# SyncE's order of transfers around the rings and up tiles of a two-layer gated kernel

## What is computed

```
x  = L0_attn_x                                     # (8, 512, 256)
xn = layernorm(x)
s  = L0_attn(xn)   # 16 query heads, 4 key groups, causal, bias -slope*sqrt(i-j), softmax
g  = silu(L0_ffn(xn))     # silu(x@W1.T) * (x@W3.T), Walsh-Hadamard, @W2.T; 1024 hidden
x  = x + s * g
xn = layernorm(x)
s  = L1_attn(xn)   # 32 causal score maps of width 8; a1 - lam*a2, rms norm, @Wo.T
g  = silu(L1_ffn(xn))     # shared expert of 352 + 8 experts of 176, top 2 by sigmoid router
x  = x + s * g
```

## Time and profile before

| | |
|---|---|
| median of 3 runs | 2348.24 us (2347.73 to 2362.52) |
| profiled execution | 2355.72 us |
| its span | 2353.8 us |
| mean granted TensorE clock | 0.963 |
| TensorE busy | 2117.3 us (90%) |
| VectorE busy | 1372.4 us (58%) |
| ScalarE busy | 893.6 us (38%) |
| GpSimd busy | 683.5 us (29%) |
| up tiles: loads, median us to landing | 176, 3.9 |
| first layer's key rings: loads, median us to landing | 32, 7.2 |

### The profile page before, as it was taken

The page is one execution under the profiler, slowest core; times in us unless marked ns, Lnnn a source line. Parts: engine busy times, 40 slices in busy tenths (PEclk is TensorE's granted clock), DMA queues, the critical chain, the costliest instruction groups (busy, mean ns, idle before and its releaser), DMA issues.

```text
span 2353.8 us, 33709 instructions
## 1 busy us (share of the span) xinstructions
PE 2117.3 (90%) x12290; PEld 1437.2 (61%) x12386; DVE 1372.4 (58%) x2691; ACT 893.6 (38%) x1749; POOL 683.5 (29%) x845
## 2 busy tenths in 40 slices
PE   2299998999989999999989999999998999989898
PEld 1157556575666656676565755757556675656656
DVE  4465655656556565556647566475565666655664
ACT  2142451425424253333524345152451425433352
POOL 2332331313313233223323233141331323322331
PEclk7589999999999999999999999999999999999999
DMA  6823423243222533116231252323422253321530
GB/s 207 287 63 101 144 68 95 72 143 100 84 70 64 166 100 104 37 55 197 85 88 54 85 166 70 102 65 121 122 78 76 72 155 102 98 51 55 173 98 14
DMA packets 105604, 240.51 MB, mean 102 GB/s; under 512 B 17048, under 2 KB 27288, under 8 KB 105184
## 3 DMA queue, kind: packets, MB, share of 16 engines
q1 hardware_dynamic: 91184, 194.41, 27.4%
q0 software_dynamic: 14256, 43.94, 6.4%
HBM read 179.67 MB, written 57.82 MB: 101 GB/s over the span
## 4 chain that ended last, share of the span: by engine, by line
PE 63%; DMA 11%; DVE 7%; SPq 4%; ACT 4%; issue 3%; POOL 2%; DVEq 0%; ACTq 0%; POOLq 0%
PE bank L387 17%; PE bank L467 11%; PE bank L546 10%; PE bank L483 9%; PE bank L436 8%; DMA upring<-up_img 3%; DMA qring<-mneg 3%; DMA k_img<-probs 3%; PE bank L440 3%; PE bank L565 2%; ACT probs L624 2%; DMA kring<-k_img 2%; SPq L334 2%; SPq L351 2%; DVE nmax L718 2%
## 5 line engine op out<-in xcount | busy, mean ns | idle before, releaser
L718 DVE TENSOR_REDUCE nmax<-bank 128x1 f32<-128x512 f32 (+3 forms) x1056 | 651.3, 639 | 366.2 <-PE bank L440 353.7
L387 PE MATMUL bank<-xnT,upring 128*128 128x512 f32 (+1 forms) x2208 | 623.8, 405 | 24.6 <-DMA upring<-up_img 23.7
L624 ACT ACTIVATE probs<-bank 128x512 f32<-128x512 f32 (+1 forms) x864 | 469.1, 560 | 345.9 <-PE bank L467 331.8
L467 PE MATMUL bank<-qring,kring 128*128 128x512 f32 (+1 forms) x1056 | 478.2, 456 | 54.6 <-ACT probs L624 24.6
L436 PE MATMUL bank<-kring,qring 127*128 127x512 f32 (+3 forms) x1536 | 461.5, 353 | 50.9 <-DMA kring<-k_img 47.4
L387 PEld LDWEIGHTS bank<-xnT,upring 128*128 128x128 f32 x2208 | 396.4, 192 | 106.2 <-issue 33.5
L436 PEld LDWEIGHTS bank<-kring,qring 127*128 127x128 f32 x1536 | 272.9, 195 | 127.3 <-DMA kring<-k_img 50.3
L546 PE MATMUL bank<-wdown,hbuf 128*128 128x256 f32 x1408 | 338.9, 391 | 0.0
L467 PEld LDWEIGHTS bank<-qring,kring 128*128 128x128 f32 x1056 | 206.3, 197 | 189.2 <-ACT probs L624 100.1
L1494 POOL TENSOR_SCALAR_AFFINE_SELECT probs<-probs 128x512 f32<-128x512 f32 x256 | 163.2, 638 | 511.5 <-ACT probs L624 509.4
L546 PEld LDWEIGHTS bank<-wdown,hbuf 128*128 128x128 f32 x1408 | 267.6, 196 | 34.9 <-issue 1.7
(11 more groups left out here) (119 smaller groups left out, 1532.3 us busy)
## 6 DMA issues: line engine op xcount, KB each, us to landing
upring<-up_img SPq DMA_DIRECT2D x176, 512.0 KB, 3.9
q_img<-probs SPq DMA_DIRECT2D x96, 256.0 KB, 4.2
qring<-q_img SPq DMA_DIRECT2D x256, 64.0 KB, 1.9
kring<-k_img SPq DMA_DIRECT2D x64, 256.0 KB, 3.1
qring<-q_img SPq DMA_DIRECT2D x32, 384.0 KB, 4.9
k_img<-probs SPq DMA_DIRECT2D x48, 256.0 KB, 4.6
up_img<-hbuf POOLq DMA_DIRECT2D x22, 512.0 KB, 4.9
gring<-gate_img POOLq DMA_DIRECT2D x32, 256.0 KB, 3.7
```

Source lines behind the costliest of these rows:

```text
L387: last = nc.tensor.matmul(out_ap, part_a(a, pa, k), part_b(b, pb, k), start=(n == 0), stop=(n == len(steps) - 1))
L467: nc.tensor.matmul(SC[n % 2][:, 0:heads * w].rearrange("p (g n) -> p g n", g=heads), kring[l][:, ks, kt * P:(kt + 1) * P], qring[l][:, s, ...
L624: nc.scalar.activation(pr, pr if biased else scores, ACT.Exp, scale=scale).then_inc(s_exp, 1)
L718: nc.vector.tensor_reduce(nmax[:, u % 2, g0:g0 + heads, qt], MX[n % 2][:, 0:heads * w].rearrange("p (g n) -> p g n", g=heads), AX.X, ALU.m ...
```

## The change

SyncE's list is put in another order at two places, and two subtractions move from GpSimd to VectorE. In the front of every batch, up tile 11 is listed ahead of ring 4, image tiles 2 and 3 are listed apart from each other with up tile 12 between, ring 5 comes behind image 3, and the max row of unit 4 comes ahead of up tiles 14 and 15. In the seven tails, image tiles 0 and 1 are listed first, then ring 0, one up tile, image 2, rings 1 and 2, and the two other up tiles. The low parts of projections 0 and 1 of the next batch are made by VectorE ahead of its copy of projection 2; GpSimd makes that of projection 2. The wait for tile 21's linear half, once for the three up tiles, stands now in `up_load_next` at its first call. What is computed stays the same.

```diff
+        def up_load_next(sp, j):
+
+            if j == 0:
+                sp.wait_ge(s_u, so_far(s_u, J_ALL - 1))
+            sp.dma_start(upring[:, j].rearrange("p a h k n -> p (a h k n)").bitcast(F32), up_img[j]).then_inc(s_uppre[j], 16)
+
...
                 up_load(sp, FRONT_TILES[0] + 2)
                 write_images(sp, 1, (0, 1))
+                up_load(sp, FRONT_TILES[1] + 2)
                 ring_load(sp, UNITS[0])
-                up_load(sp, FRONT_TILES[1] + 2)
+                write_images(sp, 1, (2,))
+                up_load(sp, FRONT_TILES[2] + 2)
+                write_images(sp, 1, (3,))
                 ring_load(sp, UNITS[0] + 1)
-                up_load(sp, FRONT_TILES[2] + 2)
-                write_images(sp, 1, (2, 3))
-                for j in FRONT_TILES[3:-1]:
+                up_load(sp, FRONT_TILES[3] + 2)
+                max_row(sp, UNITS[0])
+                for j in FRONT_TILES[4:]:
                     up_load(sp, j + 2)
-                max_row(sp, UNITS[0])
-                up_load(sp, FRONT_TILES[-1] + 2)
                 if more_batches:
                     load_x(sp, slice((b + 1) * T, (b + 2) * T))
...
                 if more_batches:
-                    sp.wait_ge(s_u, so_far(s_u, J_ALL - 1))
-                    for j in range(UP_SLOTS):
-                        sp.dma_start(upring[:, j].rearrange("p a h k n -> p (a h k n)").bitcast(F32), up_img[j])\
-                            .then_inc(s_uppre[j], 16)
-                    write_images(sp, 0, range(3))
-                    for u in RINGS_AHEAD:
-                        ring_load(sp, u)
+                    write_images(sp, 0, (0, 1))
+                    ring_load(sp, 0)
+                    up_load_next(sp, 0)
+                    write_images(sp, 0, (2,))
+                    ring_load(sp, 1)
+                    ring_load(sp, 2)
+                    for j in range(1, UP_SLOTS):
+                        up_load_next(sp, j)
...
                 dve_linear_half(dve, TILE_AFTER[U_ALL - 1])
-                for i in range(3):
+                for i in range(2):
                     dve_project(dve, 0, i)
+                project_low(nc.vector, dve, 0, 0)
+                project_low(nc.vector, dve, 0, 1)
+                dve_project(dve, 0, 2)
                 dve_normalise(dve, U_ALL - 1)
...
                 if more_batches:
-                    for i in range(3):
-                        project_low(nc.gpsimd, pool, 0, i)
+                    pool.wait_ge(s_plo[0], so_far(s_plo[0], 2))
+                    project_low(nc.gpsimd, pool, 0, 2)
```

## The result

The changed kernel takes 2335.94 us in the median of 8 runs (2330.96 to 2345.82), the kernel before, in 8 runs beside it, 2347.98 (2339.72 to 2362.52). The ratio is 0.9938, with a 95% interval of 0.9918 to 0.9957. So it is faster by 12 us between the medians, or some 15 us by the ratio, where 61 were forecast.

A forecast was written before the change was run, and what follows sets the result against it. TensorE was taken as the bound, busy nine tenths; its waits and the slow clock behind them were worth 68 us at most. Front 19 + 6.7 and tail 21.2 + 14.0 made 61, from 2348.24 to 2287 us; range 2274 to 2318.

The forecast's parts named there:

- The tail: Seven tails: ring 0 lands 3.4 us earlier, winning 21.2 us of TensorE's ring stops and 14.0 of slow clock behind them.
- `kring` won 2.8 us for 2.5, and the images 1.4 for 0.9: Tail: ring 0 without image 2 ahead lands 2.5 us sooner; images without three up tiles ahead win 0.9.
- the 2.1 us of stops that were to stay: Tail: three of seven stops exceed the 3.4 us won, by 0.8, 0.4 and 0.9, so 2.1 us stay.
- the 4.7 of bytes spread over all engines: Tail, upper bound: if image bytes used all sixteen engines, images would win 4.7 us and every tail stop would vanish.
- The cover for the two low parts: Tail: VectorE's 2.40 us idle before the last unit's reciprocal covers two low parts, 1.4 us; uncovered, 10 us in all.
- The front: Eight fronts: of 23.7 us of up tile waits, 19 are won, plus 6.7 of slow clock.
- I take 2.4, because image 2 is issued right behind ring 4 and keeps the engines fed.: Front: up tile 11 fills 2.4 us of empty DMA time, so tile 13 lands 2.4 us earlier; lower bound 1.75.
- After: the same set, ring 5 moved from the middle to just ahead of it. No byte is saved.: Front: the same transfers stand ahead of tile 13, which gets 2.4 us earlier only because work starts in empty time.
- That adds 6.7: Front: with stops below 0.9 us the clock stays up, winning 1.7 us in four of eight fronts, 6.7 in all.
- The second one: Rival: the front keeps its stop at tile 13 and gives only 8 us, the tail 35; 2305 us, chance 0.22.
- The fourth rival: Whole change: closely following transfers slow each other and both landings stay; 5 to 20 us won, 2335 us, chance 0.12.
- The slower rival: Front: ring 4 waits in SyncE's queue behind up tile 11 and lands late; 2360 us, chance 0.02.

The follow-up runs named there:

- e2: The kernel before with only the tail's new order and the two low parts on VectorE, front as before; 0.9859 of the kernel before.
- e3: e2 with all three low parts left on GpSimd; 0.9858 of the kernel before.
- e1: The kernel before with only the front's new order, tail as before; 1.0080 of the kernel before.
- e8: e2 with one transfer moved, up tile 11 ahead of ring 4; 0.9865 of the kernel before.
- e10: e5 with up tile 11 moved back behind ring 4; 0.9799 of the kernel before.
- e5: The whole change, but with ring 5 behind up tile 13 instead of ahead of it; 0.9768 of the kernel before.
- e4: The whole change with GpSimd's first gate loads of a front held until tile 13's gate half is done; 0.9994 of the kernel before.
- e9: The whole change with the second of GpSimd's two front gate loads held until tile 11 is weighed; 0.9818 of the kernel before.

## Why the prediction failed

**The tail was right.** Forecast were 21.2 us of idle and 14.0 of slow clock, 35.2; the stage gave 35.7, and e2 alone 33. In the second batch `kring` won 2.8 us for 2.5, and the images 1.4 for 0.9, so that of the 2.1 us of stops that were to stay only 1.1 did. The images won 1.4 us and not the 4.7 of bytes spread over all engines. That agrees with the rule of the Trainium skill (DMA: Bandwidth & Descriptors, section "Why a DMA increments its semaphore by 16 and not by 1") by which such images run on a few engines only. The cover for the two low parts held, and e3 shows that they weren't needed either. In all seven tails the granted clock is 1.00 over the whole stage.

**The front failed, and with its sign.** Forecast were 25.7 us won (19 idle, 6.7 clock); measured were 13.1 lost in the profile, and 19 in e1. Three steps were wrong:

- *"I take 2.4, because image 2 is issued right behind ring 4 and keeps the engines fed."* The empty 2.4 us were read as transfer time won for tile 13. e8, with tile 11's move alone, has tile 13 land as late as e2 (26.1 and 26.0 us), and e10 and e5 differ by 1.2; in the front the move is worth at most some 0.9 us. In the change the engines were busier, but for 4 us at 241 instead of 329 GB/s: a busy share is not a rate, and the traffic in the gap was another mix than what followed it before. The runs don't show which part of the mix was slow.
- *"After: the same set, ring 5 moved from the middle to just ahead of it. No byte is saved."* The count of bytes was right and was taken for a count of time. Ring 5's five issues took 3.9 us (509.23 to 513.12), where at its old place in the kernel before they took 2.1 (507.53 to 509.71), and tile 13's issue came 1.1 us later in the mean. Its transfer then ran into GpSimd's gate loads, as it did before. e5 put ring 5 behind tile 13 and won 4.2 us per front. The image split and the max row's move weren't tried alone, so the 1.1 us are not shown to be ring 5's only. The Trainium skill (DMA: Bandwidth & Descriptors, section "Issuing engines are not separate DMA queues") says that all issuers' transfers interleave on the same engines; the 0.512 and 0.385 of the two queues agree, and e4 and e9 show what it costs here: 2.7 us of tile 13's transfer. Tile 13's landing was forecast 2.4 us earlier, and came 26.9 us behind the first image's issue against 26.5 before, 0.5 later; in the mean of the eight fronts it is 26.5 against 25.9.
- *The sum for the clock, "That adds 6.7".* With a landing 0.6 us later, TensorE's earlier arrival, 0.5 us for tile 11's stop, made the stop longer by 1.1 in the mean. The working had the clock come back in the four fronts that lost it; it fell in seven. Behind the four stops of 3.3 to 4.2 us all twelve matmuls ran at 0.46 us, 2.5 us lost, where a slow front lost 1.4 to 1.6 before: 8.2 us lost in place of 6.7 won. How far a stop makes the clock fall the runs don't settle: 4.17 us in e1 was followed by matmuls at 0.36 us, 2.78 in e3 by 0.25.

**The rivals.** The second one named this place, ring 5 right ahead and gate loads at 515 to 520, and had the mechanism; but it was priced as a gain that fails to come (2305), not as a loss. It had 0.22, and set to the front's real loss it would have given 2348 - 35 + 13 = 2326 to 2348 - 35 + 19 = 2332, near the 2336 measured. The fourth rival has the number, 2335, only by chance: in it both landings stay, and ring 0's came 4.2 us earlier (2.8 and 1.4). The range ended at 2318 since no case with a tail that works and a front that loses was in it. The slower rival, ring 4 late behind tile 11, didn't happen: no front shows a stop at unit 4's first max pack.

**What would have shown it beforehand.** The profile had ring 5's transfers at a place where they were issued at 0.43 us apiece, and the parts of image 3, directly ahead of tile 13, at 3.57 us for three. It had the gate loads' stretch with 299 GB/s for both queues together, and in 515.6 to 519.0 SyncE's queue alone had 0.46 MB in 3.4 us.

## What to carry to other kernels

When a queue is the limit, a transfer that is moved needs two numbers: what stands ahead of it, and what else uses the engines at the time to which it moves. Put the transfer that is waited for first ahead of the one whose reader comes later, even if the total is the same; here one line's place was worth 30 to 40 us. When a load of another queue is held back for this, look at what stands behind its reader on the reader's engine (e4).

## What the runs showed of the hardware

- GpSimd's gate loads, 0.41 MB in 4 us, took 0.512 of the sixteen engines' time, and SyncE's 0.47 MB took 0.385. Per byte they are the dearer by about 1.5; by the figures of the kernel before in 515.6 to 519.0 (0.490 for 0.43 MB, 0.380 for 0.46) by about 1.4. With all of them held, tile 13's 512 KB landed 4.8 us after the issue, with half 6.3, with none held 7.5.
- SyncE's issue of one 64 KB ring part took 0.43 us in the mean in ring 4 (1.72 for four) and up to 1.00 in ring 5, with SyncE's own transfers at 0.798 of the engines' time and the gate loads at 0.076; this delays also what stands behind it in the program. In e4, without gate loads, ring 5's four parts still took 2.46 us.
- In the kernel before, stops of 1.88 to 1.99 us ahead of tile 13 were followed by twelve matmuls at 0.38 us, and one of 2.03 by matmuls at 0.25; behind stops of 3.3 us and more in the change they took 0.46. In e1 one of 4.17 was followed by matmuls at 0.36 and in e3 one of 2.78 by 0.25. The length of a stop alone doesn't tell what it costs.
